# A 16-head cross attention: sums behind the next subtraction, weights turned as 64-row halves, a pipeline one batch longer

## The chip, the core and the metric

The kernel runs on one core of a Trainium2 chip. The core has five engines with queues of their own: TensorE (PE, matrix products and transposes, with a separate row PEld for its weight loads), VectorE (DVE), ScalarE (ACT), GpSimd (POOL) and SyncE (SP, here only transfers). They run side by side and wait for each other by semaphores. The metric is the device time of one execution in microseconds (us). Instructions of one engine start in the order of its queue. A matrix product writes to PSUM (called `banks` here: 8 banks of 512 float32 columns), which POOL does not read.

## The reference

A decoder of some fifteen sublayers works on 32 batches of 128 tokens of width 128, with a context of 77 rows of width 96 for each batch. The change touches the two sublayers that are plain cross attentions with 16 heads of width 8, in the second and in the fourth block:

```python
q = x @ w_q + b_q                     # 32 x 128 x 128
k = context @ w_k + b_k               # 32 x 77 x 128
v = context @ w_v + b_v
# 16 heads of width 8
scores = einsum('bqhd,bkhd->bhqk', q, k) * scale
weights = softmax(scores, axis=-1)    # over the 77 context rows
out = einsum('bhqk,bkhd->bqhd', weights, v).reshape(B, Lq, D)
return out @ w_o + b_o
...
x = _layernorm(x + xattn(x, ctx), axis=-1)
```

## The kernel before

The whole decoder is one program; the sublayers stand one behind the other with a barrier between them. `xattn16` is one sublayer, called twice (`l1_xattn`, `l3_xattn`). It walks through 32 batches `t`, in eight groups `g` of four (`GB`). Inside, each engine has its own loop over the iterations `i`, and what a batch needs is spread over several iterations, so that a few batches are open at once.

For one batch, in the order of the data:

- PE: `scores(t)` (L2343), four products of 308 columns into banks 0 to 3. There is one such set of banks, so `scores(t)` waits until DVE has subtracted batch t-1.
- DVE: the maximum over the context for each head and row (L2507), then the subtraction out of PSUM into the buffer `SM` (L2511). `SM` has room for three batches.
- ACT: the exponential of `SM` in place (L2439).
- DVE: `total`, the sum over the context (L2488) and its reciprocal `RZ` (L2492).
- POOL: `normalise`, `SM` times `RZ` (L2450).
- PE: `weights_T(t, a)` for a = 0 to 3, four transposes of 128 x 77 each into one bank (L2353); banks 4 and 5 serve in turns, for the transposes and for the units below. ACT copies each set of four heads into `PT` (L2434).
- PE: `mix(t, a)`, weights times values (L2366, on a bank cleared by L2364), in bank 6 or 7. ACT copies the result to `ZT` (L2426). PE: `project(t)` (L2372), into the same bank.
- DVE: the residual, `x_res` plus the projection (L2501).

Once per group of four come: four units of PE, one in each iteration (X transposes the input, K, V and Q are products for the next group), each taken out of PSUM by ACT, for V by DVE (`values`, L2482); on POOL `group`, the output bias and the keys times a mask; and the layer norm of a finished group: statistics on DVE (L68, L72), two short instructions on ACT (L114, L116: Ln and Exp make the reciprocal deviation), and the scaling on DVE (L124, four instructions).

In DVE's loop an iteration `i` is, before: residual of batch i-4, `total(i-1)`, maximum and subtraction of batch i, then statistics, `values` or scaling where one is due. No planner is at work: the order is that of the code.

Of the kernel before, what the change touches and what calls it, by code (L numbers as in the profile page):

```python
# [2266 lines left out]
def xattn16(nc, E, prefetch=()):  # L2267
# [9 lines left out]
    with sublayer(nc, "xt_ps xt k_ps k kd v_ps v one q_ps q s_ps mx sub ex sm rz nm pt_ps pt z_ps zt o_ps rb res w_ld" + LN) as (s, ctx):  # L2277
# [3 lines left out]
        MX = sb("MX", [P, 2, H]); SM = sb("SM", [P, 3, H, L]); PT = sb("PT", [L, 2, 4, 4, P])  # L2281
# [4 lines left out]
        order = [("X", 0), ("K", 0), ("V", 0), ("Q", 0)]  # L2286
        for i in range(NB + 2):
            if i >= 2:
                order += [("T", 4 * (i - 2) + a) for a in range(4)]
            if i // GB + 1 < NG:  # L2290
                order.append(("XKVQ"[i % GB], i // GB + 1))
        place = {item: k for k, item in enumerate(order)}

        def bank_of(kind, n):
            return PS[:, 4 + place[kind, n] % 2, :]

        def bank_free(pe, kind, n):

            k = place[kind, n] - 2
            if k >= 0:  # L2300
                before, m = order[k]
                pe.wait_ge({"T": s.pt, "X": s.xt, "K": s.k, "V": s.v, "Q": s.q}[before], m + 1)

        def z_of(t):
            return PS[:, 6 + t % 2, 0:P]

        def o_of(t):
            return PS[:, 6 + t % 2, 384:384 + P]
# [6 lines left out]
        with nc.Block() as block:  # L2315
            @block.tensor
            def _(pe):
                def unit(g, u):
                    kind = "XKVQ"[u]
                    bank = bank_of(kind, g)  # L2320
                    bank_free(pe, kind, g)
# [25 lines left out]
                def weights_T(t, a):  # L2347
                    k = 4 * t + a
                    if a == 0:
                        pe.wait_ge(s.nm, t + 1)  # L2350
                    bank_free(pe, "T", k)
                    for c in range(4):
                        ins = nc.tensor.transpose(bank_of("T", k)[0:L, c * P:(c + 1) * P], SM[:, t % 3, 4 * c + a, :], E.ident)  # L2353
                    ins.then_inc(s.pt_ps, 1)

                def mix(t, a):
                    g, b = t // GB, t % GB
                    pe.wait_ge(s.pt, 4 * t + a + 1)
                    if a == 0:
                        pe.wait_ge(s.one, 1)  # L2360
                        pe.wait_ge(s.v, g + 1)
                        if t >= 2:
                            pe.wait_ge(s.res, t - 1)
                        nc.tensor.matmul(z_of(t), ZERO[:], ZERO[:], start=True, stop=False)  # L2364
                    for c in range(4):
                        ins = nc.tensor.matmul(z_of(t)[32 * c:32 * (c + 1)], value_window(g, b, 4 * c + a), PT[:, t % 2, a, c, :], start=False, stop=a == 3)  # L2366
                    if a == 3:
                        ins.then_inc(s.z_ps, 1)

                def project(t):  # L2370
                    pe.wait_ge(s.zt, t + 1)
                    nc.tensor.matmul(o_of(t), ZT[:, t % 2, :], W.wo, start=True, stop=True).then_inc(s.o_ps, 1)  # L2372
# [3 lines left out]
                for i in range(NB + 3):  # L2376
                    if i < NB:
                        scores(i)
                    t = i - 2
# [3 lines left out]
                    if 0 <= t < NB:  # L2383
                        mix(t, 0)
                        weights_T(t, 2)
                        mix(t, 1)
                        weights_T(t, 3)
                    if i // GB + 1 < NG:
                        unit(i // GB + 1, i % GB)
                    if i >= 3:  # L2390
                        project(i - 3)
                    if 0 <= t < NB:
                        mix(t, 2)
                        mix(t, 3)

            @block.scalar
            def _(act):
                nc.scalar.preload_act_table_set(EXP_LN)

                def unit(g, u):  # L2400
                    bank = bank_of("XKVQ"[u], g)
# [5 lines left out]
                    elif u == 1:  # L2407
                        act.wait_ge(s.k_ps, g + 1)
                        if g >= 2:
                            act.wait_ge(s.kd, g - 1)  # L2410
                        nc.scalar.activation(KT[:, g % 2].rearrange("p b l -> p (b l)"), bank[:, 0:CG], ACT.Identity, bias=W.bk).then_inc(s.k, 1)
                    elif u == 3:
                        act.wait_ge(s.q_ps, g + 1)
                        if g >= 2:
                            act.wait_ge(s.s_ps, GB * (g - 1))
                        nc.scalar.activation(QT[:, g % 2, :], bank, ACT.Identity, bias=W.bq).then_inc(s.q, 1)

                for u in range(4):
                    unit(0, u)
                for i in range(NB + 4):  # L2420
                    if 3 <= i < NB + 3:
                        u = i - 3
# [3 lines left out]
                        nc.scalar.copy(ZT[:, u % 2, :], z_of(u)).then_inc(s.zt, 1)  # L2426
                    t = i - 2
                    if 0 <= t < NB:
                        for a in range(4):
                            k = 4 * t + a  # L2430
                            act.wait_ge(s.pt_ps, k + 1)
                            if a == 0 and t >= 2:
                                act.wait_ge(s.z_ps, t - 1)
                            nc.scalar.copy(PT[:, t % 2, a].rearrange("p c q -> p (c q)"), bank_of("T", k)[0:L, :]).then_inc(s.pt, 1)  # L2434
                    if i // GB + 1 < NG:
                        unit(i // GB + 1, i % GB)
                    if i < NB:
                        act.wait_ge(s.sub, i + 1)
                        nc.scalar.activation(SM[:, i % 3], SM[:, i % 3], ACT.Exp, scale=float(D) ** -0.5).then_inc(s.ex, 1)  # L2439
# [4 lines left out]
            def _(pool):  # L2444
# [3 lines left out]
                def normalise(t):  # L2448
                    pool.wait_ge(s.rz, t + 1)
                    nc.gpsimd.tensor_tensor(SM[:, t % 3], SM[:, t % 3], bc(RZ[:, t % 2, :].unsqueeze(2), [P, H, L]), ALU.mult).then_inc(s.nm, 1)  # L2450
# [11 lines left out]
                for t in range(NB):  # L2462
                    normalise(t)
                    if t % GB == 1 and t // GB + 1 < NG:
# [10 lines left out]
            def _(dve):  # L2475
# [10 lines left out]
                def total(t):  # L2486
                    dve.wait_ge(s.ex, t + 1)
                    nc.vector.tensor_reduce(SU[:, t % 2, :], SM[:, t % 3], AXX, ALU.add).then_inc(s.sm, 1)  # L2488
# [6 lines left out]
                for i in range(NB + 5):  # L2495
                    if 4 <= i < NB + 4:
# [7 lines left out]
                    if i < NB:  # L2504
                        sc = PS[:, 0:4, 0:TAIL].rearrange("p a (h l) -> p a h l", l=L)
                        dve.wait_ge(s.s_ps, i + 1)
                        nc.vector.tensor_reduce(MX[:, i % 2, :].rearrange("p (a h) -> p a h", a=4), sc, AXX, ALU.max).then_inc(s.mx, 1)  # L2507
                        dve.wait_ge(s.mx, i + 1)
                        if i >= 3:
                            dve.wait_ge(s.pt_ps, 4 * (i - 2))  # L2510
                        nc.vector.tensor_tensor(SM[:, i % 3].rearrange("p (a h) l -> p a h l", a=4), sc,  # L2511
                                                bc(MX[:, i % 2, :].rearrange("p (a h) -> p a h", a=4).unsqueeze(3), [P, 4, 4, L]),
                                                ALU.subtract).then_inc(s.sub, 1)
# [4 lines left out]
                    if i < NB and i // GB + 1 < NG and i % GB == 2:  # L2518
                        values(i // GB + 1)
# [1617 lines left out]
```

## Time and profile before

| what | value |
|---|---|
| time, median of 3 runs | 3583.1 us (3573.9 to 3586.54) |
| the profiled execution | 3583.83 us, with a span of 3582.0 us |
| PE busy in the span | 2797.2 us, 78% |
| DVE busy | 2465.0 us, 69% |
| ACT busy | 1969.0 us, 55% |
| POOL busy | 1541.9 us, 43% |
| first of the two layers, 1363.4 to 1576.4 us | 213.0 us: PE 187.1, DVE 172.2, ACT 133.7, POOL 103.2 |
| second, 3217.84 to 3426.5 us | 208.66 us: PE 181.9, DVE 172.3, ACT 133.5, POOL 103.2 |

Busy time is time in which at least one instruction of the engine is under way; a share of the span is an average over all sublayers, so for this change one reads the two layers by themselves. In the rows, "a<-b" is what is written and from what, x8 the number of instructions in a row, and in square brackets stands how long the engine had stood idle before and what ended that.

### The profile page before, as it was taken

How to read it: one execution, taken by the hardware profiler on the slowest of the kernel's cores; microseconds unless marked ns; L12 is line 12 of the kernel's file. 1: busy time of each engine (PE TensorE's matmuls, PEld its weight loads, DVE VectorE, ACT ScalarE, POOL GpSimd, SP SyncE). 2: the span in 40 equal slices, each digit the busy share in tenths (PEclk: the TensorE clock that was granted, in tenths of full speed). 3: DMA queues.
4: the chain of work that ended last, by engine and by line, in shares of the span. 5: the costliest groups of instructions: out<-in, count | busy, mean ns of one | idle time of the engine just before them, and what ended most of it. 6: DMA issues, size and time to landing. Idle time of an engine off the chain costs nothing. (4 is left out here: it accounts for less than half of the span.)

```text
span 3582.0 us, 77843 instructions
## 1 busy us (share of the span) xinstructions
PE 2797.2 (78%) x28859; PEld 2018.7 (56%) x28859; DVE 2465.0 (69%) x7100; ACT 1969.0 (55%) x3803; POOL 1541.9 (43%) x1205
## 2 busy tenths in 40 slices
PE   2899999987865867989899999966655656868956
PEld 1677777655555755656455555544433446845646
DVE  6688888856555876967666676649992553568955
ACT  2577777644444754755555555545532734556747
POOL 3554555412247723520255555523221248815544
PEclk9999999999967987999999999977768858979958
DMA  4333333212102301000000000000007012300013
GB/s 136 55 54 56 56 55 53 45 59 97 49 23 66 89 27 66 2 1 1 1 2 2 2 2 2 3 1 18 19 27 217 12 41 66 95 27 20 2 32 99
DMA packets 103267, 150.94 MB, mean 42 GB/s; under 512 B 26266, under 2 KB 76524, under 8 KB 101756
## 3 DMA queue, kind: packets, MB, share of 16 engines
q1 hardware_dynamic: 91546, 123.11, 13.8%
q0 software_dynamic: 10912, 22.70, 1.9%
q8 instruction: 233, 3.82, 0.4%
q14 instruction: 142, 1.16, 0.1%
q10 hardware_dynamic: 434, 0.15, 0.0%
HBM read 81.13 MB, written 49.04 MB: 36 GB/s over the span
## 5 line engine op out<-in xcount | busy, mean ns | idle before, releaser
L458 DVE TENSOR_REDUCE MX<-banks 128x8 f32<-128x1152 f32 x128 | 173.1, 1352 | 102.1 <-PE banks L275 101.9
L2450 POOL TENSOR_TENSOR SM<-SM,RZ 128x1232 f32<-128x1232 f32 x64 | 143.8, 2248 | 194.0 <-DVE RZ L2492 192.9
L1727 POOL DMA_INDIRECT expert_results<-Y,DST x181 | 177.1, 979 | 82.0 <-issue 34.3
L1714 POOL DMA_INDIRECT sorted_rows<-SRC,IDX x160 | 156.7, 979 | 128.8 <-DVE IDX L1843 82.2
L427 POOL TENSOR_TENSOR KT<-KT,FL 128x512 f32<-128x512 f32 x64 | 81.6, 1275 | 302.6 <-DVE FL L447 302.6
L1496 PE MATMUL banks<-XC,WR 128*128 128x128 f32 x1448 | 196.7, 280 | 0.2 <-ACT XC L1616 0.2
L384 ACT COPY PT<-banks 128x384 f32<-128x384 f32 x384 | 170.3, 478 | 47.2 <-PE banks L285 43.4
L2434 ACT COPY PT<-banks 77x512 f32<-77x512 f32 x256 | 143.0, 583 | 87.1 <-PE banks L2353 84.4
L285 PE MATMUL banks<-sb_c_ident,SM 128*128 128x128 f32 x1152 | 182.6, 286 | 10.1 <-ACT PT L384 9.6
L1496 PEld LDWEIGHTS banks<-XC,WR 128*128 128x128 f32 x1448 | 179.9, 195 | 2.9 <-ACT XC L1616 2.1
L2779 POOL TENSOR_TENSOR KQ<-T,EX 128x1024 f32<-128x1024 f32 x32 | 75.9, 2372 | 235.6 <-ACT EX L2760 235.6
L471 DVE TENSOR_TENSOR SM<-banks,MX 128x512 f32<-128x512 f32 x256 | 163.4, 679 | 0.0
L2353 PE MATMUL banks<-sb_c_ident,SM 128*77 128x128 f32 x1024 | 160.5, 291 | 0.1
L1506 PE MATMUL banks<-WR,HT 128*128 128x128 f32 x1008 | 149.0, 282 | 6.8 <-DVE HT L1945 3.4
L395 ACT ACTIVATE SM<-SM 128x1152 f32<-128x1152 f32 x128 | 150.4, 1175 | 5.5 <-DVE SM L471 4.8
L285 PEld LDWEIGHTS banks<-sb_c_ident,SM 128*128 128x128 f32 x1152 | 121.5, 141 | 56.3 <-issue 25.7
L2353 PEld LDWEIGHTS banks<-sb_c_ident,SM 128*77 128x77 f32 x1024 | 114.9, 151 | 53.9 <-issue 40.0
L369 ACT ACTIVATE RAW<-banks,weight_region 128x256 f32<-128x256 f32 x256 | 108.0, 477 | 63.5 <-PE banks L256 54.3
L256 PE MATMUL banks<-XT,weight_region 128*128 128x256 f32 x512 | 137.2, 399 | 4.3 <-ACT RAW L369 3.9
L1506 PEld LDWEIGHTS banks<-WR,HT 128*128 128x128 f32 x1008 | 126.7, 191 | 14.6 <-DVE HT L1949 6.9
L59 PE MATMUL banks<-sb_c_ident,x_res 128*128 128x128 f32 x256 | 47.5, 330 | 111.7 <-PEq L48 111.7
L1635 ACT ACTIVATE HT<-banks,WR 128x128 f32<-128x128 f32 x284 | 81.4, 368 | 95.0 <-PE banks L1496 94.2
(565 smaller groups left out, 8604.8 us busy)
## 6 DMA issues: line engine op xcount, KB each, us to landing
FL<-RAW SPq DMA_DIRECT2D x512, 64.0 KB, 2.3
sorted_rows<-in_zeros_dram SPq DMA_DIRECT2D x33, 528.0 KB, 8.6
XR<-sorted_rows SPq DMA_DIRECT2D x181, 66.0 KB, 1.9
SRC<-expert_results SPq DMA_DIRECT2D x16, 512.0 KB, 7.8
T<-s4d_k_dram SPq DMA_DIRECT2D x8, 1024.0 KB, 10.3
weight_region<-in_l_ffn__wall_dram SPq DMA_DIRECT2D x1, 4112.0 KB
film_dram<-F SPq DMA_DIRECT2D x8, 512.0 KB, 2.9
FO<-film_dram SPq DMA_DIRECT2D x8, 512.0 KB, 5.1
```

The source lines that it names most:

```text
L285: ins = nc.tensor.transpose(ring(item, n)[:, q * P:(q + 1) * P], SM[:, n % 3, 3 * c + q, :], E.ident)
L384: nc.scalar.copy(PT[:, n % 2, 3 * c:3 * c + 3, :].rearrange("p h q -> p (h q)"), ring(f"T{c}", n)[:, 0:3 * P]).then_inc(s.pt, 1)
L395: nc.scalar.activation(SM[:, (n - 1) % 3], SM[:, (n - 1) % 3], ACT.Exp, scale=SCALE).then_inc(s.ex, 1)
L458: nc.vector.tensor_reduce(MX[:, n % 2], sc, AXX, ALU.max).then_inc(s.mx, 1)
L471: nc.vector.tensor_tensor(main[:, h:h + 2], sc[:, h:h + 2, :, 0:P], bc(MX[:, n % 2, h:h + 2].unsqueeze(3), [P, 2, 2, P]), ALU.subtract).th ...
L1496: ins = nc.tensor.matmul(up_bank(j, c // 2)[:, (c % 2) * P:(c % 2 + 1) * P], w[:, at * P:(at + 1) * P], XC[:, j % 2, :], start=True, stop= ...
L1506: ins = nc.tensor.matmul(down_bank(j), HT[:, j % 2, c, :], w[:, c * P:(c + 1) * P], start=c == 0, stop=c == hb - 1)
L1714: nc.gpsimd.indirect_dma_start(out=rows, out_offset=bass.IndirectOffsetOnAxis(ap=IDX[:, k, t:t + 1], axis=0), in_=SRC[:, t, k, :], in_offs ...
L1727: nc.gpsimd.indirect_dma_start(out=results, out_offset=bass.IndirectOffsetOnAxis(ap=DST[:, j % ST:j % ST + 1], axis=0), in_=Y[:, j % ST, : ...
L2353: ins = nc.tensor.transpose(bank_of("T", k)[0:L, c * P:(c + 1) * P], SM[:, t % 3, 4 * c + a, :], E.ident)
L2434: nc.scalar.copy(PT[:, t % 2, a].rearrange("p c q -> p (c q)"), bank_of("T", k)[0:L, :]).then_inc(s.pt, 1)
L2450: nc.gpsimd.tensor_tensor(SM[:, t % 3], SM[:, t % 3], bc(RZ[:, t % 2, :].unsqueeze(2), [P, H, L]), ALU.mult).then_inc(s.nm, 1)
```

## The change

Five things change in `xattn16`, and nothing outside it.

1. DVE's loop: maximum and subtraction of batch i now come first, then `values` where due, then `total(i-1)`, then the residual of batch i-4, then statistics or scaling.
2. The pipeline is one iteration longer: weights of batch i-3 (before: i-2) are turned in iteration i, `SM` has four places in place of three, and POOL's `group` comes one batch earlier.
3. The weights are turned in two parts of eight heads. Each part is 16 transposes of 64 rows, rows 0 to 63 into bank 4 and rows 64 to 127 into bank 5 in turns; ACT takes both banks with one copy of 1024 columns. The next part waits for that copy.
4. The banks have fixed tasks: 4 and 5 the transposes, 6 the mix, 7 the projection and the units. Units of the next groups wait until the one before was taken and, from iteration 5 on, for the residual of batch i-5.
5. The units come in the order X, K, Q, V.

```diff
-        MX = sb("MX", [P, 2, H]); SM = sb("SM", [P, 3, H, L]); PT = sb("PT", [L, 2, 4, 4, P])
+        MX = sb("MX", [P, 2, H]); SM = sb("SM", [P, 4, H, L]); PT = sb("PT", [L, 2, 4, 4, P])
...
+        HALF = (slice(0, 64), slice(64, 128))
+        UNITS = "XKQV"
+        turned = PS[0:L, 4:6, :].rearrange("k r (h q) -> k h r q", q=64)
+        z_bank, o_bank = PS[:, 6, 0:P], PS[:, 7, 0:P]
...
                 def weights_T(t, a):
-                    k = 4 * t + a
                     if a == 0:
                         pe.wait_ge(s.nm, t + 1)
-                    bank_free(pe, "T", k)
-                    for c in range(4):
-                        ins = nc.tensor.transpose(bank_of("T", k)[0:L, c * P:(c + 1) * P], SM[:, t % 3, 4 * c + a, :], E.ident)
+                    if 2 * t + a >= 1:
+                        pe.wait_ge(s.pt, 2 * t + a)
+                    for k in range(8):
+                        for r in range(2):
+                            ins = nc.tensor.transpose(turned[:, k, r, :], SM[HALF[r], t % 4, 4 * (k % 4) + 2 * a + k // 4, :], E.ident[HALF[r], HALF[r]])
                     ins.then_inc(s.pt_ps, 1)
...
+                for i in range(NB + 4):
+                    t = i - 3
+                    more = i // GB + 1 < NG
+                    if i < NB:
+                        scores(i)
+                    if 0 <= t < NB:
+                        weights_T(t, 0)
+                    if more:
+                        if i == 0:
+                            taken(pe, "V", 0)
+                        elif i < 5:
+                            taken(pe, UNITS[(i - 1) % GB], (i - 1) // GB + 1)
+                        else:
+                            pe.wait_ge(s.res, i - 4)
+                        unit(i // GB + 1, i % GB)
+                    if 1 <= t <= NB:
+                        mix(t - 1, 1)
+                    if 0 <= t < NB:
+                        weights_T(t, 1)
+                        mix(t, 0)
+                    if 1 <= t <= NB:
+                        if more:
+                            taken(pe, UNITS[i % GB], i // GB + 1)
                         if t >= 2:
                             pe.wait_ge(s.res, t - 1)
...
+                        project(t - 1)
...
+                def weights(t, a):
+                    act.wait_ge(s.pt_ps, 2 * t + a + 1)
+                    if a == 0 and t >= 2:
+                        act.wait_ge(s.z_ps, t - 1)
+                    nc.scalar.copy(PT[:, t % 2, 2 * a:2 * a + 2].rearrange("k q c (r p) -> k (q c) r p", r=2), turned).then_inc(s.pt, 1)
...
                 for i in range(NB + 5):
+                    if i < NB:
+                        sc = PS[:, 0:4, 0:TAIL].rearrange("p a (h l) -> p a h l", l=L)
+                        dve.wait_ge(s.s_ps, i + 1)
...
+                    if i < NB and i // GB + 1 < NG and UNITS[i % GB] == "V":
+                        values(i // GB + 1)
+                    if 1 <= i <= NB:
+                        total(i - 1)
                     if 4 <= i < NB + 4:
                         t = i - 4
                         dve.wait_ge(s.o_ps, t + 1)
                         if t % GB == 0:
                             dve.wait_ge(s.rb, t // GB + 1)
-                        nc.vector.tensor_tensor(XB[:, t, :], o_of(t), XB[:, t, :], ALU.add).then_inc(s.res, 1)
-                    if 1 <= i <= NB:
-                        total(i - 1)
...
+                        nc.vector.tensor_tensor(XB[:, t, :], o_bank, XB[:, t, :], ALU.add).then_inc(s.res, 1)
                     if i >= 7 and (i - 7) % GB == 0:
```

On ACT the order in an iteration is now: copy of the first part of batch i-3, the unit's copy, `ZT` of batch i-4, copy of the second part, exponential of batch i, and in every fourth iteration the two norm instructions.

The first place is DVE's queue around a scaling, in the middle of a layer. Before, from a subtraction (L2511) to the reciprocal behind the scaling:

```order
L2511 TENSOR_TENSOR SM<-banks,MX 128x1232
L68 BN_STATS ln_stats<-x_res 128x6 x4
L72 BN_AGGR ln_mv<-ln_stats 128x2 x4
L2501 TENSOR_TENSOR x_res<-banks,x_res 128x128
L2488 TENSOR_REDUCE SU<-SM 128x16
L2492 RECIPROCAL RZ<-SU 128x16
L2507 TENSOR_REDUCE MX<-banks 128x16
L2511 TENSOR_TENSOR SM<-banks,MX 128x1232
L124 TENSOR_SCALAR x_res<-x_res,ln_mv,ln_rstd 128x128 x4
L2501 TENSOR_TENSOR x_res<-banks,x_res 128x128
L2488 TENSOR_REDUCE SU<-SM 128x16
L2492 RECIPROCAL RZ<-SU 128x16
```

With the change, from right behind a subtraction to the scaling (the lines of the changed file are: L2497 maximum, L2501 subtraction, L2486 sum, L2490 reciprocal, L2513 residual, L2480 values):

```order
L2480 TENSOR_TENSOR VZ<-banks,weight_region 77x64x8
L2486 TENSOR_REDUCE SU<-SM 128x16
L2490 RECIPROCAL RZ<-SU 128x16
L2513 TENSOR_TENSOR x_res<-banks,x_res 128x128
L68 BN_STATS ln_stats<-x_res 128x6 x4
L72 BN_AGGR ln_mv<-ln_stats 128x2 x4
L2497 TENSOR_REDUCE MX<-banks 128x16
L2501 TENSOR_TENSOR SM<-banks,MX 128x1232
L2486 TENSOR_REDUCE SU<-SM 128x16
L2490 RECIPROCAL RZ<-SU 128x16
L2513 TENSOR_TENSOR x_res<-banks,x_res 128x128
L124 TENSOR_SCALAR x_res<-x_res,ln_mv,ln_rstd 128x128 x4
```

The sum, the reciprocal and the residual moved from ahead of the maximum to behind the subtraction; with them the statistics and the scaling moved from directly behind a subtraction to behind a reciprocal and a residual, and `values` came into the same iteration as the statistics.

The second place is PE's queue in one iteration, from the scores of a batch to the next scores. Before (the unit here is V, L2329):

```order
L2343 MATMUL banks<-KD,QT 128x308 x4
L2353 MATMUL banks<-sb_c_ident,SM 77x128 x8
L2364 MATMUL banks<-zero 128x128
L2366 MATMUL banks<-PT,VZ 32x128 x4
L2353 MATMUL banks<-sb_c_ident,SM 77x128 x4
L2366 MATMUL banks<-PT,VZ 32x128 x4
L2353 MATMUL banks<-sb_c_ident,SM 77x128 x4
L2329 MATMUL banks<-weight_region,ctx_T 77x128 x4
L2372 MATMUL banks<-weight_region,ZT 128x128
L2366 MATMUL banks<-PT,VZ 32x128 x8
```

With the change (L2329 scores, L2340 transposes, L2311 the unit K, L2354 mix, L2351 its clearing, L2360 projection):

```order
L2329 MATMUL banks<-KD,QT 128x308 x4
L2340 MATMUL banks<-sb_c_ident,SM 77x64 x16
L2311 MATMUL banks<-ctx_T,weight_region 128x308
L2354 MATMUL banks<-PT,VZ 32x128 x8
L2340 MATMUL banks<-sb_c_ident,SM 77x64 x16
L2351 MATMUL banks<-zero 128x128
L2354 MATMUL banks<-PT,VZ 32x128 x8
L2360 MATMUL banks<-weight_region,ZT 128x128
```

Three spells of transposes became two, each of 16 instructions with half the columns; the unit went to between the first spell and the mix, and the projection to the end.

## Rows read from the trace of the kernel before

**Rows 1.** Busy us (instructions) of PE, PEld, DVE, ACT, POOL; PE's clock; DMA; GB/s.

```profile
1385.00:1400.00 15.00, 15.00 (x109) 9.39 (x107) 6.47 (x7) 6.52 (x10) 6.25 (x4) 0.54 0.00 1
1400.00:1562.00 162.00, 149.83 (x1752) 99.33 (x1748) 146.24 (x223) 113.01 (x199) 83.64 (x40) 1.00 0.01 2
2790.00:2870.00 80.00, 55.20 (x252) 35.22 (x252) 42.17 (x174) 58.49 (x116) 18.41 (x25) 0.85 0.02 7
```

**Rows 2.** Timeline, DVE and ACT, one batch: start us, us, engine, line, operation.

```profile
1553.82 1.44 DVE L2511 TENSOR_TENSOR SM<-banks,MX 128x1232 f32<-128x1232 f32 x1
...
1555.17 0.28 DVE L2501 TENSOR_TENSOR x_res<-banks,x_res 128x128 f32<-128x128 f32 x1
1555.29 1.23 ACT L2439 ACTIVATE SM<-SM 128x1232 f32<-128x1232 f32 x1 [0.96 <-DVE SM L2511]
...
1556.55 1.44 DVE L2488 TENSOR_REDUCE SU<-SM 128x16 f32<-128x1232 f32 x1 [1.10 <-ACT SM L2439]
...
1558.02 0.25 DVE L2492 RECIPROCAL RZ<-SU 128x16 f32<-128x16 f32 x1
1558.19 1.38 DVE L2507 TENSOR_REDUCE MX<-banks 128x16 f32<-128x1232 f32 x1
...
1559.61 1.44 DVE L2511 TENSOR_TENSOR SM<-banks,MX 128x1232 f32<-128x1232 f32 x1
```

**Rows 3.** Timeline, beginning and end of both layers: first, ninth subtraction, second scores, last copy.

```profile
1372.99 1.44 DVE L2511 TENSOR_TENSOR SM<-banks,MX 128x1232 f32<-128x1232 f32 x1
...
1374.48 1.41 PE L2343 MATMUL banks<-KD,QT 32*128 32x308 f32 x8 [1.98 <-DVE SM L2511]
...
1426.42 1.44 DVE L2511 TENSOR_TENSOR SM<-banks,MX 128x1232 f32<-128x1232 f32 x1
...
1570.14 0.58 ACT L2434 COPY PT<-banks 77x512 f32<-77x512 f32 x1 [0.37 <-PE banks L2353]
...
3228.06 1.44 DVE L2511 TENSOR_TENSOR SM<-banks,MX 128x1232 f32<-128x1232 f32 x1
...
3275.23 1.44 DVE L2511 TENSOR_TENSOR SM<-banks,MX 128x1232 f32<-128x1232 f32 x1
```

**Rows 4.** Timeline, DVE, batches with values, with statistics and with the scaling.

```profile
1439.35 0.68 DVE L2482 TENSOR_TENSOR VZ<-banks,weight_region 77x512 f32<-77x512 f32 x1
...
1445.14 0.86 DVE L68 BATCH_NORM_STATS2 ln_stats<-x_res 128x6 f32<-128x128 f32 x4
...
1446.34 0.26 DVE L2501 TENSOR_TENSOR x_res<-banks,x_res 128x128 f32<-128x128 f32 x1
...
1446.52 1.44 DVE L2488 TENSOR_REDUCE SU<-SM 128x16 f32<-128x1232 f32 x1
...
1450.93 1.11 DVE L124 TENSOR_SCALAR x_res<-x_res,ln_mv,ln_rstd 128x128 f32<-128x128 f32 x4
```

**Rows 5.** Timeline, DVE and POOL, the scaling in the drain of the first layer.

```profile
1563.82 0.25 DVE L2492 RECIPROCAL RZ<-SU 128x16 f32<-128x16 f32 x1
1563.99 3.01 DVE L124 TENSOR_SCALAR x_res<-x_res,ln_mv,ln_rstd 128x128 f32<-128x128 f32 x4
...
1564.15 2.25 POOL L2450 TENSOR_TENSOR SM<-SM,RZ 128x1232 f32<-128x1232 f32 x1 [3.54 <-DVE RZ L2492]
...
1566.91 0.28 DVE L2501 TENSOR_TENSOR x_res<-banks,x_res 128x128 f32<-128x128 f32 x1
```

**Rows 6.** Page, costliest groups (busy us, mean ns); timeline, PE in the gated layer.

```profile
L2434 ACT COPY PT<-banks 77x512 f32<-77x512 f32 x256 | 143.0, 583 | 87.1 <-PE banks L2353 84.4
...
L2353 PE MATMUL banks<-sb_c_ident,SM 128*77 128x128 f32 x1024 | 160.5, 291 | 0.1
...
1905.99 0.22 PE L2664 MATMUL banks<-sb_c_ident,KQ 64*64 64x64 f32 x1
...
1906.71 0.22 PE L2665 MATMUL banks<-VA,KQ 64*64 64x64 f32 x1
```

More of the change, by code:

```diff
@@ L2284, in xattn16, with bank_of, taken @@
         XB = E.x
[L2286 to L2308, printed above, removed]
+        HALF = (slice(0, 64), slice(64, 128))
+        UNITS = "XKQV"
+        turned = PS[0:L, 4:6, :].rearrange("k r (h q) -> k h r q", q=64)
+        z_bank, o_bank = PS[:, 6, 0:P], PS[:, 7, 0:P]
+        def bank_of(kind, g):
+            return PS[:, 7 if g else 4 + UNITS.index(kind), :]
+        def taken(pe, kind, g):
+            pe.wait_ge({"X": s.xt, "K": s.k, "V": s.v, "Q": s.q}[kind], g + 1)
         def value_window(g, b, h):
@@ L2361, in mix @@
                         pe.wait_ge(s.v, g + 1)
[L2362 to L2367, printed above, removed]
+                        if t >= 1:
+                            pe.wait_ge(s.zt, t)
+                        nc.tensor.matmul(z_bank, ZERO[:], ZERO[:], start=True, stop=False)
+                    for q in (2 * a, 2 * a + 1):
+                        for c in range(4):
+                            ins = nc.tensor.matmul(z_bank[32 * c:32 * (c + 1)], value_window(g, b, 4 * c + q), PT[:, t % 2, q, c, :], start=False, stop=q == 3)
+                    if a == 1:
                         ins.then_inc(s.z_ps, 1)
@@ L2371, in project @@
                     pe.wait_ge(s.zt, t + 1)
-                    nc.tensor.matmul(o_of(t), ZT[:, t % 2, :], W.wo, start=True, stop=True).then_inc(s.o_ps, 1)
+                    nc.tensor.matmul(o_bank, ZT[:, t % 2, :], W.wo, start=True, stop=True).then_inc(s.o_ps, 1)
                 for u in range(4):
                     unit(0, u)
-                for i in range(NB + 3):
+                for i in range(NB + 4):
+                    t = i - 3
+                    more = i // GB + 1 < NG
                     if i < NB:
                         scores(i)
-                    t = i - 2
                     if 0 <= t < NB:
                         weights_T(t, 0)
+                    if more:
[9 more added lines that the diff above has]
+                    if 0 <= t < NB:
                         weights_T(t, 1)
-                    if 0 <= t < NB:
                         mix(t, 0)
[L2385 to L2394, printed above, removed]
+                    if 1 <= t <= NB:
+                        if more:
+                            taken(pe, UNITS[i % GB], i // GB + 1)
+                        if t >= 2:
+                            pe.wait_ge(s.res, t - 1)
+                        project(t - 1)
             @block.scalar
@@ L2400, in unit @@
                 def unit(g, u):
-                    bank = bank_of("XKVQ"[u], g)
+                    bank = bank_of(UNITS[u], g)
                     if u == 0:
@@ L2419, in _ @@
                     unit(0, u)
-                for i in range(NB + 4):
-                    if 3 <= i < NB + 3:
-                        u = i - 3
+                def weights(t, a):
[3 more added lines that the diff above has]
+                    nc.scalar.copy(PT[:, t % 2, 2 * a:2 * a + 2].rearrange("k q c (r p) -> k (q c) r p", r=2), turned).then_inc(s.pt, 1)
+                for i in range(NB + 4):
+                    t = i - 3
+                    if 0 <= t < NB:
+                        weights(t, 0)
+                    if i // GB + 1 < NG:
+                        unit(i // GB + 1, i % GB)
+                    if 1 <= t <= NB:
+                        u = t - 1
                         act.wait_ge(s.z_ps, u + 1)
@@ L2425, in _ @@
                             act.wait_ge(s.o_ps, u - 1)
-                        nc.scalar.copy(ZT[:, u % 2, :], z_of(u)).then_inc(s.zt, 1)
-                    t = i - 2
+                        nc.scalar.copy(ZT[:, u % 2, :], z_bank).then_inc(s.zt, 1)
                     if 0 <= t < NB:
[L2429 to L2436, printed above, removed]
+                        weights(t, 1)
                     if i < NB:
                         act.wait_ge(s.sub, i + 1)
-                        nc.scalar.activation(SM[:, i % 3], SM[:, i % 3], ACT.Exp, scale=float(D) ** -0.5).then_inc(s.ex, 1)
+                        nc.scalar.activation(SM[:, i % 4], SM[:, i % 4], ACT.Exp, scale=float(D) ** -0.5).then_inc(s.ex, 1)
                     if i >= 7 and (i - 7) % GB == 0:
@@ L2463, in _ @@
                     normalise(t)
-                    if t % GB == 1 and t // GB + 1 < NG:
+                    if t % GB == 0 and t // GB + 1 < NG:
                         group(t // GB + 1)
```

30 lines of the change are left out of this document (12 added, 18 removed).

## Prediction

> **What bounds the kernel now.** I read the page first (two layers run the changed function, with the same 64 batches in all), then busy times by stretch, then the timeline of single batches. Between 1400 and 1562 us of the first layer 28 batches pass: VectorE (DVE) is busy 146.2 of 162 us, TensorE (PE) 149.8, and PE has its full 2.4 GHz [rows 1]. Both look full, so shares alone decide nothing; the order of time does. From one subtraction of a batch to the next, 1553.82 to 1559.61, pass 5.79 us [rows 2], and the next sub starts from 1426.42 (the ninth) to 1559.61 (the 32nd) are 133.19 us for 23 batches, again 5.79 [rows 2, 3]. The ring is on two engines: subtraction, exponential on ACT 1.23, then DVE's sum, reciprocal, maximum, next subtraction. DVE stands 1.10 us before the sum until ACT's exponential ends, with only the residual put into the hole [rows 2]. What else DVE does (values, statistics, scaling of the layer norm) goes into that hole: in the batch with the statistics the sum starts with no wait at 1446.52 [rows 4]. So PE is not the bound; the exponential that DVE waits for is a link of the ring.
>
> **The change, part by part.** *Sums a batch later.* The sum of batch i-1 now stands behind the subtraction of batch i, when its exponential is long done. The ring without ACT, from starts to starts: subtraction 1.35, sum 1.47, reciprocal 0.17, maximum 1.42 [rows 2], residual at most 0.18 (1446.34 to 1446.52) [rows 4]: 4.59 us. But what filled the hole is no longer free. Per four batches: four rings 18.36, values 0.68, statistics 1.20 plus 0.1 because they now read what the residual just wrote, scaling 1.11 less 0.08 overlap, 1.03 [rows 4]: 21.4, against 4 x 5.79 = 23.16.
>
> *The scaling meets GpSimd.* The scaling (L124, four tensor_scalar) stood behind the subtraction, when POOL was idle; now it stands behind reciprocal and residual, and the reciprocal is what starts POOL's normalisation of 2.25 us. Before has this meeting in the drain: reciprocal at 1563.82, scaling 1563.99, POOL 1564.15 to 1566.40, and the scaling takes 3.01 us in place of 1.11, with the next DVE start 0.51 us behind POOL's end [rows 5]. Now POOL starts 0.33 after the reciprocal's start and the scaling 0.35, so all four may have to wait: 2.58 (POOL's end) + 0.51 + 0.26 for the one more - 0.35 = 3.0 in place of 1.03, 1.97 more. Bounds: 1.89 (the row: 2.92 - 1.03) to 2.23 (held to POOL's very end). A group of four is then 23.4 against 23.16: **in the steady part nothing is gained**, 0.2 us per group is lost.
> The Trainium skill, SBUF — State Buffer, section "Who interferes with whom", says that a DVE instruction in a two-port mode, tensor_scalar among them, and a GpSimd instruction exclude each other, and whichever starts first holds the port pair for its whole instruction. By it the scaling would wait POOL's remaining 2.23 us: 12 scalings x 0.26 = 3 us more than my sum. The row shows the wait, but some of the four got in before; the sum above goes by the row.
>
> *Where the gain is.* Scaling begins with the ninth batch, so the first eight are free of it. Sub 0 stands at 1372.99 and 3228.06, sub 8 at 1426.42 and 3275.23 [rows 3]: 53.4 and 47.2 us. After: PE is at half clock there (0.54 from 1385 to 1400 [rows 1]); scores take 1.41 behind the subtraction [rows 3], so the first three steps are 1.44 + 0.05 + 1.41 + 0.06 + 1.42 = 4.4 each, 13.1. The next two, in which PE starts on weights with its clock still low, are between 4.59 (DVE) and 8.4 (twice PE's warm work, below); I take 6.0, nearer to DVE, since much of PE's time is latency. Then two of 4.59 and one with values and statistics, 6.6. Sum 40.9: gains of 12.5 and 6.3 us; 9 to 15 and 4 to 9 by when the clock rises.
> Batches 8 to 28, five groups: -1.0 per layer. The last three steps: 3 x 4.59 + 3.0 = 16.8 against 17.4, +0.6.
>
> *Weights turned as halves.* PE before: 149.8/28 = 5.35 us per batch [rows 1], of which 160.5/64 = 2.5 are 16 transposes of 128 columns [rows 6]. After: two spells of 16 transposes of 64 columns, rows 0-63 and 64-127 in turns into two banks. Bounds: where the gated layer uses four 64-row tiles in turns, starts repeat tile by tile every 0.06 us, 52 between 1905.99 and 1906.71, each 0.22 long [rows 6]: 8 x 0.06 + 0.2 = 0.7 per spell if the two tiles run side by side; 16 x 0.06 + 0.2 = 1.2 if not. I take 0.7, being the row for alternating tiles: PE 5.35 - 2.5 + 1.4 = 4.2 per batch, under 4.59. Its scores may come 0.9 us late before the maximum waits, as sum, reciprocal and residual (1.8) lie between. So PE's saving itself is worth nothing in the steady part: it keeps PE from becoming the bound.
> ACT copies 1024 columns in one: 583 ns for 512 [rows 6] and 1.23 us for 1232 [rows 2] give 0.9 ns a column, 1.04 us; two copies for four save 0.25 us a batch, off the path.
>
> *New waits.* PE's unit waits for the residual of five batches ago (1.9 us behind the subtraction), with half the mix, the second spell and the projection queued behind; these 2 us still fit. ACT's Ln and Exp for the norm now wait for statistics that stand behind the sum, some 3.6 us after the subtraction, and the copy of the next batch's first half is queued behind them: 3.6 + 0.5 + 1.04, then second spell, mix and projection 1.7, makes 6.9 against DVE's 6.6. PE is 0.3 us late, inside the 0.9. POOL's bias and mask product (moved one batch forward) end before the batch that needs them.
>
> *The drain.* One batch more is open when the last subtraction ends, and weights use only one pair of banks, so turning and copying alternate. From the last subtraction (T = 1559.61): the sum of batch 30 and the reciprocal 1.35 + 1.47 + 0.17, residual 0.3, statistics 1.2, so ACT is free at about T + 5.0 after its two norm instructions (0.5, estimate). Then the copy of batch 29's first half 1.04, and five more halves of 0.7 + 1.04 + 0.05 = 1.8: T + 15.0. Before, the last copy ended at 1570.14 + 0.58 = T + 11.1 [rows 3]. The rest is the same. 3.9 us lost per layer, 8 in both; 12 if spells take 1.2.
>
> *The clock.* In batches with the scaling DVE needs 7.6 us and PE 4.7, so PE stands 2.9 us once per four batches; now it is busy 92% of this stretch [rows 1]. Another stretch, where it is busy 55.2 of 80 us, has a mean clock of 0.85 [rows 1]. I put in 0.2 us a group, 2.5 us in both layers; from 0 to 6.
>
> **Sum.** 12.5 + 6.3 - 2 x 1.0 + 2 x 0.6 - 8 - 2.5 = 7.5 us less than the profiled execution's 3583.83, which is 0.7 above the median: 3575.5 us.
>
> **The rivals.** *The scaling does not wait* (POOL is later than I think, or DVE takes the port first): 2 x 6 x 1.97 = 23.6 less, 3552. For it: seven of the eight scalings in each layer now take 1.11. Against: the row of 3.01 has the very neighbours that all will have.
> *PE becomes the bound, its clock falls*: this one ends slower. If PE waits 2.9 us in each group and the clock stays at 1.2 GHz after it, a batch costs PE about 6.2 (4.2 warm, half of it doubling), over DVE's mean of 5.85: (6.2 - 5.85) x 24 x 2 = 17 us, and spells at half clock in the drain add 0.5 x 5 x 2 = 5: 3598. It decides from about half of the batches at the low clock on. For it: 0.54 and 10.5-us batches at the start; against: 1.00 for 162 us with more transposes, and a PE that is late is a PE that is busy.
> *The halves do not run side by side*: PE 5.2 per batch, more than 4.59 in two of four, hidden by the long ones; the drain costs 4 more, the cold start 3: 3582.
> A change without any effect cannot be, as the order on DVE is another; but gain and loss may cancel, which lies inside my forecast.
>
> **Chances.** Three runs of before lie 0.35% apart, so a measurement tells about 0.3%, 10.7 us, from no change. Forecast 0.54 (3566 to 3585: faster 0.21, same 0.33); scaling does not wait 0.12 (faster); halves in series 0.12 (same 0.09, slower 0.03); clock 0.14 (slower 0.12, same 0.02); something not seen 0.08 (faster 0.05, slower 0.03). Together faster 0.38, same 0.44, slower 0.18. Range 3554 to 3595: it leaves out the far side of the first rival and of the clock.
>
> **What the profile after would show.** Subtractions 4.6 us apart in two of four batches, 6.6 and 7.6 in the others, and 4.4 at the start; DVE without idle time from the first to the last; L124 at about 3 us, seven times per layer; transposes in spells of 0.7; copies of 1.04; the last copy some 15 us behind the last subtraction. It would be wrong if the scaling stays at 1.1, if spells take over 1.2, if the sum still waits for ACT, or if the maximum waits for PE.

## The result and the profile after

The changed kernel takes 3638.5 us (median of four, 3634.6 to 3657.0) against 3583.2: the ratio is 1.0169, with a 95% interval of 1.0129 to 1.0208. It is **slower by some 55 us**, 43 us above the end of my range. The profiled execution took 3636.79 us, with a span of 3635.0.

Lines of the changed kernel: L2329 scores, L2340 transposes, L2419 their copy, L2354 mix, L2360 projection, L2497 maximum, L2501 subtraction, L2486 sum, L2490 reciprocal, L2513 residual.

First the busy times by stretch (columns as in [rows 1]); the third row answers to the 162 us at 1.00 of before:

```profile
1435.00:1454.00 19.00, 15.07 (x260) 10.39 (x253) 17.49 (x27) 12.35 (x18) 6.31 (x3) 1.00 0.01 2
1479.00:1481.00 2.00, 2.00 (x21) 1.62 (x18) 1.97 (x4) 0.90 (x2) 1.26 (x1) 0.50 0.03 8
1497.00:1542.00 45.00, 45.00 (x424) 28.41 (x423) 32.86 (x45) 21.45 (x28) 19.86 (x10) 0.50 0.01 2
1575.00:1600.00 25.00, 20.98 (x250) 14.92 (x248) 8.44 (x31) 10.04 (x16) 4.49 (x2) 0.50 0.01 1
3276.00:3304.00 28.00, 24.07 (x407) 16.11 (x399) 26.89 (x39) 19.62 (x28) 14.64 (x7) 1.00 0.01 2
3347.00:3369.00 22.00, 22.00 (x202) 13.53 (x201) 15.55 (x19) 10.72 (x13) 10.18 (x5) 0.50 0.01 1
```

Between 1497 and 1542 PE is at 1.2 GHz although it is busy in 45.00 of 45 us, and DVE, which should set the pace, is busy in 32.86. Read the rows at 1.00 against those at 0.50, leaving out the drain (from 1575): PE's busy share is lower where the clock is high.

Where the clock is up, DVE does what was predicted. Its timeline around a scaling, with POOL's row (answers to [rows 4, 5]):

```profile
1471.78 0.25 DVE L2490 RECIPROCAL RZ<-SU 128x16 f32<-128x16 f32 x1
1471.94 0.23 DVE L2513 TENSOR_TENSOR x_res<-banks,x_res 128x128 f32<-128x128 f32 x1
1472.09 3.12 DVE L124 TENSOR_SCALAR x_res<-x_res,ln_mv,ln_rstd 128x128 f32<-128x128 f32 x4
...
1472.11 2.25 POOL L2448 TENSOR_TENSOR SM<-SM,RZ 128x1232 f32<-128x1232 f32 x1 [3.65 <-DVE RZ L2490]
...
1475.13 1.43 DVE L2497 TENSOR_REDUCE MX<-banks 128x16 f32<-128x1232 f32 x1
1476.59 1.44 DVE L2501 TENSOR_TENSOR SM<-banks,MX 128x1232 f32<-128x1232 f32 x1
...
1481.18 1.44 DVE L2501 TENSOR_TENSOR SM<-banks,MX 128x1232 f32<-128x1232 f32 x1
```

Meanwhile PE stands still, since the scores wait for that subtraction, and right behind this wait the clock is 0.50, from 1479 to 1481 (rows above). PE's timeline ahead of that, there, through one batch at 1.00 (V's unit, 4.87 us from scores to scores), ahead of the long stretch at 0.50, and through one batch in it, again with V's unit:

```profile
1460.13 0.80 PE L2329 MATMUL banks<-KD,QT 32*128 32x308 f32 x8
1460.86 0.77 PE L2340 MATMUL banks<-sb_c_ident,SM 64*77 64x64 f32 x16
...
1478.09 1.04 PE L2329 MATMUL banks<-KD,QT 32*128 32x308 f32 x8 [2.46 <-DVE SM L2501]
...
1484.56 0.80 PE L2329 MATMUL banks<-KD,QT 32*128 32x308 f32 x8
...
1489.43 0.80 PE L2329 MATMUL banks<-KD,QT 32*128 32x308 f32 x8
...
1493.55 0.77 PE L2340 MATMUL banks<-sb_c_ident,SM 64*77 64x64 f32 x16 [1.46 <-ACT PT L2419]
...
1512.19 1.41 PE L2329 MATMUL banks<-KD,QT 32*128 32x308 f32 x8
1513.53 1.30 PE L2340 MATMUL banks<-sb_c_ident,SM 64*77 64x64 f32 x16
1514.76 1.99 PE L2315 MATMUL banks<-weight_region,ctx_T 96*77 96x128 f32 x8
1516.68 1.08 PE L2354 MATMUL banks<-PT,VZ 77*32 77x128 f32 x16
1517.69 1.30 PE L2340 MATMUL banks<-sb_c_ident,SM 64*77 64x64 f32 x16
1518.92 0.28 PE L2351 MATMUL banks<-zero 1*128 1x128 bf16 x1
1519.14 1.08 PE L2354 MATMUL banks<-PT,VZ 77*32 77x128 f32 x16
1520.15 0.80 PE L2360 MATMUL banks<-weight_region,ZT 128*128 128x128 f32 x2
1520.88 1.41 PE L2329 MATMUL banks<-KD,QT 32*128 32x308 f32 x8
```

The wait of 1.46 us is another than the one behind the scaling: the second spell waits for ACT's copy of the first, which stands behind the two norm instructions. The long fall comes behind this wait: the clock is 1.00 from 1483 to 1495 and 0.50 from 1496 on, ahead of the next scaling:

```profile
1483.00:1495.00 12.00, 10.54 (x193) 7.51 (x189) 10.91 (x20) 8.36 (x13) 6.89 (x4) 1.00 0.01 1
1496.00:1542.00 46.00, 46.00 (x432) 28.75 (x427) 33.82 (x48) 21.95 (x29) 20.31 (x10) 0.50 0.01 2
...
1496.53 3.12 DVE L124 TENSOR_SCALAR x_res<-x_res,ln_mv,ln_rstd 128x128 f32<-128x128 f32 x4
```

Once up, the clock falls ten times in the two layers as long as scores are made, each time in a PE wait of 1.46 to 2.47 us or within 2.4 us of its end; four more such waits have no fall behind them.

In the batch from 1512.19, 8.69 us pass from scores to scores without a gap: PE is now the bound. DVE's waits from 1497 to 1542 (us in total, times, longest) name PE each time:

```profile
DVE x_res L2513 <- PE banks L2360: 7.6, 4, 2.9
DVE MX L2497 <- PE banks L2329: 2.8, 3, 1.1
DVE VZ L2480 <- PE banks L2354: 1.3, 1, 1.3
```

Where the time went, from the timeline of DVE, both layers added up: stretches between subtractions by their number (0 to 31), and from the last one to the end of the layer norm. The two right columns are experiments told below.

| stretch, us | before | after | full rows | full rows, scaling first |
|---|---|---|---|---|
| subtraction 0 to 8 | 100.6 | 90.7 | 82.5 | 81.0 |
| 8 to 28 | 231.6 | 274.8 | 238.2 | 219.7 |
| 28 to 31 | 34.7 | 40.3 | 33.7 | 29.8 |
| 31 to the end of the norm | 33.0 | 54.6 | 44.2 | 44.2 |
| sum | 400.0 | 460.4 | 398.6 | 374.7 |

The two layers lose 60.4 us; the spans differ by 53.0 since outside the table this execution was 7.4 us shorter, 3.9 of it ahead of the first subtraction (1369.08 against 1372.99). For the first layer after, the anchors are these rows, the others are read in the same way:

```profile
1369.08 1.44 DVE L2501 TENSOR_TENSOR SM<-banks,MX 128x1232 f32<-128x1232 f32 x1
...
1418.15 1.44 DVE L2501 TENSOR_TENSOR SM<-banks,MX 128x1232 f32<-128x1232 f32 x1
...
1506.37 1.44 DVE L2501 TENSOR_TENSOR SM<-banks,MX 128x1232 f32<-128x1232 f32 x1
...
1547.01 1.44 DVE L2501 TENSOR_TENSOR SM<-banks,MX 128x1232 f32<-128x1232 f32 x1
1553.50 1.44 DVE L2501 TENSOR_TENSOR SM<-banks,MX 128x1232 f32<-128x1232 f32 x1
...
1573.66 1.44 DVE L2501 TENSOR_TENSOR SM<-banks,MX 128x1232 f32<-128x1232 f32 x1
...
1599.82 1.12 DVE L124 TENSOR_SCALAR x_res<-x_res,ln_mv,ln_rstd 128x128 f32<-128x128 f32 x4 [0.60 <-ACT ln_rstd L116]
```

From 1506.37 to 1547.01 five batches take 8.13 us each.

### The profile page after: what moved, and what is told of

The parts are those of the page before. It is cut to its first block and busy times, and to the rows that moved or that the text cites. A ratio compares the mean times of both kernels' runs of the same rounds, so it can differ in the third digit from the quotient of the medians.

```text
span 3635.0 us, 79823 instructions
## 1 busy us (share of the span) xinstructions
PE 2858.9 (79%) x29883; PEld 2056.3 (57%) x29883; DVE 2483.7 (68%) x7100; ACT 1955.4 (54%) x3675; POOL 1542.0 (42%) x1205
## 5 line engine op out<-in xcount | busy, mean ns | idle before, releaser
L2419 ACT COPY PT<-banks 77x1024 f32<-77x1024 f32 x128 | 128.9, 1007 | 124.9 <-PE banks L2340 124.9
L2340 PEld LDWEIGHTS banks<-sb_c_ident,SM 64*77 64x77 f32 x2048 | 115.8, 200 | 75.7 <-issue 45.1
L2340 PE MATMUL banks<-sb_c_ident,SM 64*77 64x64 f32 x2048 | 136.7, 294 | 18.1 <-ACT PT L2419 17.2
```

What stands on the lines that cost most here:

```text
L2340: ins = nc.tensor.transpose(turned[:, k, r, :], SM[HALF[r], t % 4, 4 * (k % 4) + 2 * a + k // 4, :], E.ident[HALF[r], HALF[r]])
```

## The experiments

Three theories: **H1**, the stalled scaling opens a gap of 2.5 us on PE, and the gap drops the clock. **H2**, the clock drops because the halves leave PE's array less to do per batch. **H3**, the new order waits by itself at any clock. All kernels but one are the changed kernel with the edit shown.

**Halves undone.**

```diff
-    for k in range(8):
-        for r in range(2):
-            ins = nc.tensor.transpose(turned[:, k, r, :], SM[HALF[r], ...], E.ident[HALF[r], HALF[r]])
+    for k in range(8):
+        ins = nc.tensor.transpose(whole[:, k, :], SM[:, ...], E.ident)
...
-    nc.scalar.copy(PT[...].rearrange("k q c (r p) -> k (q c) r p", r=2), turned).then_inc(s.pt, 1)
+    nc.scalar.copy(PT[...].rearrange("k q c p -> k (q c) p"), whole).then_inc(s.pt, 1)
```

(`whole` is the same two banks, seen as eight transposes of 128 columns.)

> The changed kernel with eight transposes of all 128 rows per spell in place of sixteen of 64 rows; same copy of 1024 columns, same order. H1: the stalled scaling is still there and so is TensorE's wait of 2.5 us; the clock still falls after it; 3620 us or more. H2 (less work for TensorE lets the clock fall): more array time per batch, clock 1.0 apart from single dips, about 3585 us. H3: no change, 3630 to 3640 us.

Measured: 3584.4 us, ratio to before 1.0006 (0.9996 to 1.0016). Its busy times, and its timeline of a scaling and of the scores behind it (lines are one lower here):

```profile
1400.00:1490.00 90.00, 82.07 (x983) 56.70 (x976) 87.33 (x126) 59.83 (x82) 49.62 (x24) 1.00 0.01 2
...
1440.56 3.12 DVE L124 TENSOR_SCALAR x_res<-x_res,ln_mv,ln_rstd 128x128 f32<-128x128 f32 x4
...
1446.56 0.80 PE L2329 MATMUL banks<-KD,QT 32*128 32x308 f32 x8 [1.62 <-DVE SM L2500]
1447.29 1.10 PE L2339 MATMUL banks<-sb_c_ident,SM 128*77 128x128 f32 x8
```

The scaling still takes 3.12 us and PE still waits behind it, but the clock stays at 1.00, apart from one short fall in each layer (at 1494 and 3368, each at the end of a wait of 1.61 us), and all that the change lost comes back. H3 falls: the order is the same. H1 is not yet out, since more work on PE also shortens its waits: the gap shrank to 1.62 us, and the wait for ACT's copy to 0.77.

**Scaling first**, so that it meets no normalisation and opens no gap:

```diff
                     ... ALU.subtract).then_inc(s.sub, 1)
+                    if i >= 8 and (i - 8) % GB == 0:
+                        dve_ln_scale(...)
                     if i < NB and ... UNITS[i % GB] == "V":
                         values(i // GB + 1)
                     if 1 <= i <= NB:
                         total(i - 1)
...
-                    if i >= 8 and (i - 8) % GB == 0:
-                        dve_ln_scale(...)
```

> The changed kernel with the scaling of the layer norm directly behind the subtraction, as in the kernel before, so that it no longer meets GpSimd's normalisation. H1 (the clock falls because the stalled scaling makes TensorE wait 2.5 us for the next subtraction): scaling 1.11 us, group of four 21.4 us, clock 1.0 once it has risen, 3545 to 3565 us. H2 (the clock falls because TensorE has less to do per batch): DVE paces faster still, TensorE at 1.2 GHz in long stretches, steps of 7 to 9 us there, 3600 us or more. H3 (the new order on TensorE and ACT waits by itself, at any clock): steps above 5 us also where the clock is 1.0, 3590 to 3625 us.

Measured: 3626.9 us, ratio 1.0104 (1.0064 to 1.0144). Its busy times in the first layer and in the one long stretch of the second with its clock up:

```profile
1400.00:1472.00 72.00, 72.00 (x684) 46.44 (x681) 45.84 (x69) 34.26 (x45) 29.78 (x15) 0.50 0.01 2
3297.00:3339.00 42.00, 38.27 (x645) 25.66 (x645) 40.53 (x62) 30.98 (x43) 24.79 (x12) 1.00 0.01 2
```

Without the stall the clock is at half for even longer in the first layer, with PE busy 72.00 of 72 us. That it is longer is not shown to be the edit's doing: the stretch begins ahead of the first scaling (1424.22), where the two kernels do the same. **H1 falls** as it was put: the gap of 2.5 us can go with a fall, as at 1479 after, but taking it away does not keep the clock. What the edit leaves is PE's wait for ACT's copy, and in the second layer the clock falls behind that one, to stay low with PE busy all the time:

```profile
3338.07 0.77 PE L2340 MATMUL banks<-sb_c_ident,SM 64*77 64x64 f32 x16 [1.48 <-ACT PT L2419]
...
3341.00:3353.00 12.00, 12.00 (x111) 7.18 (x111) 9.54 (x11) 5.53 (x8) 7.93 (x4) 0.50 0.01 1
```

In the stretch from 3297 to 3339 groups take 21.3 us (21.4 expected). The time is not clearly below the changed kernel's: the intervals of the two ratios overlap.

**The sum back ahead of the maximum**, where it also keeps the scaling clear of POOL:

```diff
                 for i in range(NB + 5):
+                    if 1 <= i <= NB:
+                        total(i - 1)
                     if i < NB:
...
-                    if 1 <= i <= NB:
-                        total(i - 1)
```

> The changed kernel with the sum of the batch back ahead of the next maximum; pipeline length, halves and their order stay. The scaling then comes 2.8 us or more after the reciprocal, when POOL is done. H1: no stalled scaling, no wait of 2.5 us on TensorE; ring of 5.79 us, clock 1.0 after the start, 3580 to 3600 us. H2: TensorE has 4.2 us of work in 5.79, less of its time busy than in the changed kernel, so the clock is low at least as long; 3640 us or more. H3: same as the changed kernel or a little more, 3630 to 3650 us.

Measured: 3682.9 us, ratio 1.0289 (1.0259 to 1.0319), the slowest so far:

```profile
1400.00:1445.00 45.00, 45.00 (x420) 28.90 (x421) 28.87 (x42) 21.00 (x28) 18.88 (x10) 0.50 0.00 1
```

No scaling stalls, and the time is far from what H1 and H3 gave; it is as H2 says. But the edit also brings PE a wait of its own, 1.75 us for `values` (at 1455.19), with a fall of the clock behind it, so this run does not tell less work from more waiting.

**Each spell of half transposes twice**, more work with the same output:

```diff
-                    for k in range(8):
+                    for k in (*range(8), *range(8)):
```

> The changed kernel with each spell of sixteen half transposes issued twice, so that TensorE's transposing doubles (0.77 us more per spell warm) and nothing else changes. H2: the added work keeps the clock up; steps of 8 to 9 us go, and the kernel is faster than the changed one, 3590 to 3620 us. H1 and H3: the clock falls as before and each cold spell is 1.3 us longer; slower than the changed kernel, 3670 to 3720 us.

Measured: 3604.4 us, ratio 1.0058 (1.0037 to 1.0078). Doing the transposes twice makes the changed kernel 34 us *faster*, though not as fast as before. The wait behind the scaling shrinks with it, to 0.84 us (at 1458.01). Its busy times:

```profile
1408.00:1554.00 146.00, 140.39 (x2693) 103.27 (x2689) 138.73 (x198) 92.56 (x125) 74.39 (x36) 1.00 0.01 3
```

**Halves in series**, to tell occupied time from amount of work:

```diff
-                    for k in range(8):
-                        for r in range(2):
+                    for r in range(2):
+                        for k in range(8):
```

> The changed kernel with each spell's eight transposes of rows 0 to 63 ahead of its eight of rows 64 to 127, so that the two halves of the array don't alternate; same sixteen instructions. H2a (what keeps the clock is how long TensorE's array is occupied): a spell is about 1.1 to 1.2 us warm as with full rows, the clock stays up, 3584 to 3600 us. H2b (what keeps it is how much of the array is at work, rows times columns): the same work as in the changed kernel in more time, the clock is as low or lower, 3635 to 3680 us.

Measured: 3790.4 us, ratio 1.0576 (1.0561 to 1.0591), far beyond both. Its busy times:

```profile
1400.00:1520.00 120.00, 120.00 (x1003) 82.55 (x998) 70.24 (x103) 49.58 (x66) 38.12 (x19) 0.50 0.00 1
```

One of its spells in the timeline:

```profile
1452.52 1.88 PE L2340 MATMUL banks<-sb_c_ident,SM 64*77 64x64 f32 x16
```

That is 1.88 us in place of 1.30 at this clock. PE never stands, four batches take 38 us, and the clock is at 0.50 from 1371 to 1687, through the whole first layer. So PE being occupied does not raise it (H2a falls), and no wait of PE is needed to keep it low. H2b had the direction; I had its size wrong, since I had not seen that a PE that is the bound at 1.2 GHz can stay there.

**Less work in the kernel before**, whose order and transposes stay:

```diff
-                    for c in range(4):
+                    for c in range(2):
                         ins = nc.tensor.transpose(bank_of("T", k)..., SM[:, t % 3, 4 * c + a, :], E.ident)
```

> The kernel before, its order untouched, with eight of the sixteen weight transposes of each batch left out (heads whose rows stay what the bank last held), so that only TensorE's work falls, by about 1.25 us a batch. H2 (too little array work drops the clock): the clock falls in the steady part, a batch costs TensorE about 8 us in place of 5.79, and the kernel is slower with less to do: 3620 to 3710 us. Otherwise (the fall belongs to the new order or to side-by-side halves): the ring over DVE and ACT keeps its 5.79 us, 3573 to 3585 us.

Measured: 3615.6 us, ratio 1.0104 (1.0082 to 1.0126), just under what H2 gave (3620 to 3710) and far above the other (3573 to 3585): the clock falls in some stretches only. Its busy times:

```profile
1400.00:1450.00 50.00, 40.30 (x478) 23.29 (x471) 44.93 (x69) 35.26 (x63) 25.57 (x13) 1.00 0.01 2
1542.00:1560.00 18.00, 17.51 (x140) 9.37 (x141) 14.08 (x18) 9.57 (x16) 6.17 (x3) 0.50 0.00 1
```

With less to do it is slower, with no half, no longer pipeline and, ahead of the drain, no stalled scaling in it. This and the doubled spells show from both sides that the clock hangs on PE's work. In both, PE's waits change along with the work (here ACT's copy is waited for 0.91 us, at 1444.12, where before shows 0.47, at 1447.68), so they don't tell whether a fall starts from the wait or from there being less work. That a wait keeps the clock low is ruled out by the stretches at 0.50 with PE busy all the time.

**Combinations**: scaling first with full rows, with doubled halves, and with full rows in the first spell and halves in the second.

> The changed kernel with transposes of all 128 rows and with the scaling directly behind the subtraction, both at once. H2 (the halves take from TensorE the work that keeps its clock up; the stalled scaling costs only its own 2 us): clock 1.0 from the sixth batch on, group of four 21.4 us in place of 23.55, so 6 groups x 2 layers x 2.15 = 26 us less than with full rows alone: 3558 us, 3550 to 3566. If TensorE, with about 5.3 us a batch, becomes the bound at full clock: groups of 22 to 22.5, 3565 to 3575 us. H1 (gaps of TensorE decide): nothing left to make a gap, 3550 to 3566 as well, but then it would have had to be slow with full rows alone.

> The changed kernel with the scaling directly behind the subtraction and each spell of half transposes issued twice. The scaling first alone left TensorE at half clock for 106 us although it was busy without a gap; if it is the small work per batch (H2), twice the transposes bring the clock back: groups of about 22 to 23.5 us (TensorE some 5.8 us a batch), 3570 to 3595 us. If not (another wait of the new order), more work can only make it slower than with the scaling first alone: 3640 to 3700 us.

> The changed kernel with the scaling directly behind the subtraction, the first spell of each batch as eight transposes of 128 rows and the second as sixteen half transposes: half way between scaling first alone (3627) and scaling first with full rows (3557). H2 as a matter of amount: either the clock holds and the time is that of full rows or 2 to 4 us less (3550 to 3562), or it falls in some stretches (3575 to 3610). If it is the mere presence of 64-row tiles that drops the clock: near 3627.

Measured: full rows 3557.1 us, ratio 0.9927 (0.9911 to 0.9943); doubled halves 3586.7, ratio 1.0020 (1.0008 to 1.0032); one spell of halves 3554.5, ratio 0.9927 (0.9909 to 0.9946). Busy times in this order:

```profile
1400.00:1530.00 130.00, 124.33 (x1497) 86.49 (x1497) 124.58 (x192) 89.76 (x125) 74.01 (x36) 1.00 0.01 2
```

```profile
1408.00:1530.00 122.00, 121.86 (x2329) 90.00 (x2327) 111.85 (x171) 80.12 (x109) 64.87 (x32) 1.00 0.01 3
```

```profile
1455.00:1460.00 5.00, 5.00 (x63) 3.59 (x59) 4.93 (x6) 2.56 (x5) 2.25 (x1) 0.69 0.00 0
...
1459.00:1519.00 60.00, 55.40 (x813) 38.41 (x809) 58.29 (x94) 42.94 (x60) 34.96 (x17) 1.00 0.01 2
```

The first and the third **beat both kernels**, and can't be told apart. Full rows with the scaling first is 27 us under full rows alone; the table has 23.9 of it from subtraction 0 to 31 (354.4 against 330.5). Groups of four take 21.97 us (21.4 expected) in place of 23.55: the scaling's step loses 2.0, another grows from 4.83 to 5.27. Ten groups give 15.8, the last three steps of both layers 3.9, the short falls that don't come 2.7, the start 1.5. The third keeps its clock but for short falls (at 1410, 1455 and 1520 in the first layer, each behind a PE wait of 1.1 us or more), so 64-row tiles as such do not hold it down. Doubled halves make PE itself the bound at full clock: 121.86 of 122 us.

## Why the prediction was wrong

**The step that failed** is the price of the halves. I wrote that PE's saving "is worth nothing in the steady part: it keeps PE from becoming the bound". It cost the clock, and by that made PE the bound. The term that was mis-sized is the allowance for the clock: 2.5 us in the sum, 0 to 6 as its bounds; after less full rows is 460.4 - 398.6 = 62 us over the two layers (54 in the medians).

- *The rival with the clock* had the right end (3598 forecast, 3638 measured), but for another cause and at too low a price. I let PE's wait of 2.9 us drop the clock (2.46 measured). Falls do stand behind it; but the scaling put first took the wait away, and the clock fell all the same, behind a wait that I had not priced for the clock: under *New waits* I had the copy behind the norm instructions as 0.3 us late and hidden from DVE. Hidden it is, but PE stands 1.46 us for it. I priced a cold batch at 6.2 us, doubling only half of PE's work; five batches measured 8.13 each, and the rows show that not half but nearly all of it grows by about 1.7: spells from 0.77 to 1.30, scores from 0.80 to 1.41, a batch with V's unit from 4.87 to 8.69. That "much of PE's time is latency", on which I went at the start of the layer too, does not hold in these rows; the 8.4 us that I gave there as the upper bound of such a batch was near. And "a PE that is late is a PE that is busy", my argument against it, is true and of no help: 45.00 of 45 us busy at 0.50.
- *The ring without ACT*: 4.59 us predicted, 1476.59 to 1481.18 measured. Right.
- *The scaling*: 3.0 us predicted, 3.04 measured to the next start. All four instructions waited for POOL: 0.77 us from POOL's end (1474.36) to the next start (1475.13) is my 0.51 + 0.26. The Trainium skill, SBUF — State Buffer, section "Who interferes with whom", says that whichever of the two issues first holds the port pair for its whole instruction and the other blocks; the wait agrees, while who issued first the records can't tell, as they show starts, the scaling's 0.02 us ahead of POOL's.
- *The first eight batches*: gains of 12.5 and 6.3 predicted; with full rows, so with the clock up, 53.4 - 41.5 = 11.9 and 47.2 - 41.0 = 6.2. The sum is right, in part by luck: the two cold steps for which I took 12 measured 11.2 and 10.7, the two after them 10.5 in place of 9.2. The changed kernel itself kept 4.4 and 5.6.
- *Groups of four*: 23.4 predicted; 23.55 with full rows. Eight to 28 lost 3.3 per layer there in place of 1.0: 2.0 from the groups (23.55 - 23.16, five times), the rest where one longer step (6.24 and 6.15 for 4.83) meets a short fall of the clock.
- *Halves, copies*: 0.77 us a spell for 0.7, 1.01 a copy for 1.04. Right. But the 2.5 us for PE's transposes of before was too much: full rows take 2 x 1.10 per batch. Against them the saving on PE is 0.66 us a batch, not 1.1, which leaves an estimate of 5.35 - 0.66 = 4.7 us a batch in place of 4.2: no longer under DVE's 4.59.
- *The drain*: 3.9 us per layer predicted; 6.3 and 4.9 with full rows (22.1 against 15.8 and 17.2), 11.5 and 10.1 in the changed kernel, whose spells run at half clock there (1575 to 1600, above). Mis-sized in both: with full rows the first copy starts 5.0 us behind the last subtraction, as forecast, but the five halves behind it take 2.2 us each in place of 1.8, and 2.7 in the changed kernel.

The kernel with full rows is level with before: 18.1 won at the start and 1.1 in the last three steps, 6.6 and 11.2 lost in between and in the drain (table), 1.4 in all. Without its allowance for the clock the forecast had 10.0; 4.6 of the difference lies in the groups and 3.2 in the drain. What was left to win lay in the scaling's meeting with POOL, whose stall I had priced rightly.

**What stays open**: which measure of PE's work sets the clock, and what part PE's short waits have in a fall. The runs order the cases; they do not give the measure, and none takes all of PE's waits away with the work left as it is.

## What to carry to other kernels

Before taking work from a TensorE that runs near its bound, ask whether its clock is part of the balance: here turning all weights as halves, or only half of the weights, lost more to 1.2 GHz than it saved, and repeating the halves won part of that back. A busy share did not show it; read the granted clock beside it, and what PE waited for ahead of each fall, and test by adding harmless work. An instruction with a neighbour on GpSimd is worth moving by itself: put directly behind the subtraction, the scaling was worth 27 us where the clock was up.

## What the runs showed of the hardware

- PE can stay at 1.2 GHz with no idle time at all: 72.00 of 72, 120.00 of 120 us busy at 0.50, while 40.30 of 50 us went at 1.00 in the kernel with fewer transposes. With the halves in series it stayed there from 1371 to 1687.
- In the steady part of the changed kernel the clock fell in or just behind PE waits of 1.46 to 2.47 us, ten times out of fourteen such waits. With full rows two of twelve waits of some 1.6 us had one, and it was short.
- Transposes count towards the clock here: leaving out eight of sixteen dropped it in stretches, doubling the halves restored it. The Trainium skill, TensorE: Matmul & The Clock Gate, section "Part 4: PE-mode transpose", says that they do not count as PE-busy in the same way and that the full clock does not engage for them. The second these runs contradict, as spells ran at 1.00 and more of them brought the clock back; whether they count as much as other products no run here shows.
- Two tiles of 64 rows in turns run side by side, to judge by the times: sixteen half transposes took 0.77 us at 2.4 GHz and 1.30 at 1.2; at 1.2 GHz one half behind the other took 1.88.
